# A folded bias in a graph convolution: one-row products on TensorE, or a multiply-add on VectorE from spread sums

## The reference, cut to what matters

```python
src, dst, norm = _gcn_norm(edge_index, N)      # norm = dinv[src] * dinv[dst], self loops added
h = x @ W_ae + b_ae                            # 3125 x 256 -> 3125 x 512
h = sigmoid(_gcn_conv(h, src, dst, norm, W1, b1, N))   # 512 -> 512
h = sigmoid(_gcn_conv(h, src, dst, norm, W2, b2, N))   # 512 -> 256

def _gcn_conv(h, src, dst, norm, W, b, n):
    hw = h @ W
    msg = norm[:, None] * hw[src]
    return segment_sum(msg, dst, num_segments=n) + b
```

## Time and profile before

| | before |
|---|---|
| median of 3 runs | 4179.58 us (4172.24 to 4185.87) |
| the profiled execution's own time | 4175.88 us |
| its span in the trace | 4174.1 us |
| busy: PE / PEld | 3630.8 us (87%) / 2671.5 us (64%) |
| busy: DVE / ACT / POOL | 2214.6 us (53%) / 1380.5 us (33%) / 701.9 us (17%) |
| mean granted TensorE clock | 0.92 |

### The profile page before, as it was taken

How to read it: one execution, slowest core, us unless ns; L and a number is a source line. 1 busy time by engine, 2 the same in 40 slices (tenths; PEclk the granted TensorE clock), 3 DMA queues, 4 the chain that set the end, 5 groups by cost and what they waited for, 6 DMA issues and landing times. The chain is left out here.

```text
span 4174.1 us, 91756 instructions
## 1 busy us (share of the span) xinstructions
PE 3630.8 (87%) x23927; PEld 2671.5 (64%) x23978; DVE 2214.6 (53%) x5682; ACT 1380.5 (33%) x3071; POOL 701.9 (17%) x1302
## 2 busy tenths in 40 slices
PE   4888867499979999999999997599998998799998
PEld 2444434266648967977778665498895444577776
DVE  6988877888880012115577634502106777433333
ACT  2555651377770021023210332301101253233333
POOL 3221100000000000001466632000004663000000
PEclk9999995588879998999899998699999999899999
DMA  3112220132224502520221222353351000100000
GB/s 114 46 74 79 87 110 26 41 91 84 87 78 163 195 39 102 208 91 20 73 56 49 43 64 102 125 204 123 135 206 51 1 1 5 26 8 15 12 10 31
DMA packets 121971, 320.85 MB, mean 77 GB/s; under 512 B 39597, under 2 KB 71836, under 8 KB 106554
## 3 DMA queue, kind: packets, MB, share of 16 engines
q1 hardware_dynamic: 108476, 302.94, 20.6%
q0 software_dynamic: 9936, 9.42, 1.5%
q10 hardware_dynamic: 3410, 6.54, 0.4%
HBM read 246.05 MB, written 72.96 MB: 76 GB/s over the span
## 5 line engine op out<-in xcount | busy, mean ns | idle before, releaser
L559 PE MATMUL ps<-hot_key,hot_src 128*126 128x512 bf16 (+1 forms) x2208 | 413.4, 313 | 75.7 <-DVE hot_key L524 47.4
L524 DVE TENSOR_SCALAR hot_key<-col_iota,run_keys 128x625 bf16<-128x625 int16 x1104 | 394.0, 378 | 0.0
L559 PEld LDWEIGHTS ps<-hot_key,hot_src 128*126 128x126 bf16 x2208 | 215.2, 137 | 264.7 <-DVE hot_key L524 183.0
L1365 PE MATMUL ps<-gnn_u_thirds,near 125*128 125x256 bf16 x3000 | 336.0, 275 | 13.7 <-issue 13.7
L1365 PEld LDWEIGHTS ps<-gnn_u_thirds,near 125*128 125x128 bf16 x3000 | 330.4, 141 | 16.5 <-issue 14.5
L521 DVE TENSOR_SCALAR hot_src<-col_iota,run_srcs 128x125 bf16<-128x125 int16 x828 | 212.4, 256 | 67.3 <-PE ps L559 29.1
L3773 DVE SCALAR_TENSOR_TENSOR xres<-ps,shares,xres 125x256 f32 x200 | 96.8, 484 | 244.1 <-PE ps L3738 223.3
L868 PE MATMUL ps<-row_hot,slot_hot 128*128 128x512 f16 x1088 | 221.5, 357 | 2.2 <-DVE row_hot L1081 2.2
L2542 PE MATMUL ps<-xnT,ew 128*128 (+2 forms) x640 | 181.8, 437 | 25.4 <-ACT ehT L2651 15.8
L2557 PE MATMUL ps<-ew,ehT 128*125 128x256 f32 x800 | 201.9, 396 | 0.0
L3727 PE MATMUL ps<-xnT,f 128*128 x640 | 184.6, 436 | 12.3 <-ACTq L3746 4.7
(11 more groups left out here) (595 smaller groups left out, 6743.6 us busy)
## 6 DMA issues: line engine op xcount, KB each, us to landing
near<-adjacency SPq DMA_DIRECT2D x80, 1562.5 KB, 6.5
adjacency<-counts SPq DMA_DIRECT2D x125, 312.5 KB, 2.2
own_in<-own_rows SPq DMA_DIRECT2D x34, 512.0 KB, 4.0
expert_rows<-rows_y SPq DMA_DIRECT2D x75, 125.0 KB
rows_room<-expert_rows SPq DMA_DIRECT2D x25, 375.0 KB
pair_in<-high_rows SPq DMA_DIRECT2D x34, 256.0 KB, 4.8
pair_in<-low_rows SPq DMA_DIRECT2D x34, 256.0 KB, 5.4
rows_room<-key_rows SPq DMA_DIRECT2D x8, 1024.0 KB
```

The source lines that it names most:

```text
L524: nc.vector.tensor_scalar(hot_key[:, j, :], col_iota[:], run_keys[:, ds(at, 1), j:j + 1].rearrange("p a j -> p (a j)"), None, ALU.is_equal ...
L559: last = nc.tensor.matmul(sums[:, b:e], hot_src[:, j, :], hot_key[:, j, b:e], start=False, stop=True, skip_group_check=True)
L1365: last = nc.tensor.matmul(ps[:, j, 0:width], lead_tiles[BUF[j]][:, k, :], parts.thirds[:, k, i, :], start=(k == 0 and i == 0), stop=(k == ...
```

## The change

1. `folded.b` becomes four columns on 128 partitions instead of one row of 512. PE makes them with 16 products that have `W1` as weights (128x128) and one moving column (line 665 of the changed kernel) in place of 4 products with 512 columns.
2. Ahead of the loop over groups, the node sums are spread over all partitions. DVE writes a row of 128 ones; PE multiplies it by `sT` in ten products with one row of weights (the ten halves); ACT copies the even ones and DVE the odd ones out of PSUM into `spare[:, ...]`. PE and DVE wait until all ten are out before they enter the loop.
3. In the loop the one-row product is gone. DVE adds the bias in PSUM, in place: piece += sums x folded bias (one `scalar_tensor_tensor`, 40 in all). ACT's sigmoid waits for DVE instead of PE.
4. Pieces take banks 0, 1 and 7 in turn, and a piece waits until ACT has done the one that last had its bank (`PIECE_BACK`, counted in pieces).

```diff
-        folded_b = folding.enter_context(nc.sbuf_tensor("b_ae_w1", [1, HID], F32))
+        folded_b = folding.enter_context(nc.sbuf_tensor("b_ae_w1", [128, 4], F32))
...
-                for k in range(4):
-                    last = nc.tensor.matmul(ps[0:1, 7, :], self.b_ae[:, k:k + 1], self.w1[:, k, :], start=(k == 0),
-                                            stop=(k == 3))
+                for m in range(4):
+                    for k in range(4):
+                        last = nc.tensor.matmul(ps[:, 7, m:m + 1], self.w1[:, k, m * 128:(m + 1) * 128], self.b_ae[:, k:k + 1],
+                                                start=(k == 0), stop=(k == 3))
...
-                nc.scalar.activation(self.b[:], ps[0:1, 7, :], ACT.Copy).then_inc(self.folded_out, 1)
+                nc.scalar.activation(self.b[:], ps[:, 7, 0:4], ACT.Copy).then_inc(self.folded_out, 1)
...
+                    SPREADS = [(g * NG + first, n) for g in range(G) for first, n in HALVES]
+                    SPREAD_BANKS = 6
+                    PIECE_BANK = (0, 1, 7, 0, 1, 7, 0, 1)
+                    PIECE_BACK = (2, 2, 5, 3, 3, 3, 3, 3)
+
+                    def spread_of(i):
+                        return ps[:, 2 + i % SPREAD_BANKS, 0:SPREADS[i][1]]
...
                         pe.wait_ge(landed, 32)
+                        pe.wait_ge(one_made, 1)
+                        for i, (first, n) in enumerate(SPREADS):
+                            if i >= SPREAD_BANKS:
+                                pe.wait_ge(spread_out[i % 2], (i - SPREAD_BANKS) // 2 + 1)
+                            nc.tensor.matmul(spread_of(i), one_row[:], sT[0:1, first:first + n], start=True,
+                                             stop=True).then_inc(spread_done, 1)
+                        for i in range(2):
+                            pe.wait_ge(spread_out[i], G)
                         with pe.Fori(0, G) as g:
...
-                                    pe.wait_ge(piece_out, g * 8 + (piece + 1))
-                                    o = ps[:, piece % 2, 0:n]
+                                    pe.wait_ge(piece_out, g * 8 + (piece + 9 - PIECE_BACK[piece]))
+                                    o = ps[:, PIECE_BANK[piece], 0:n]
...
-                                        nc.tensor.matmul(o, folded.w[:, c, cols], aggT[:, c, ds(g * NG + first, n)],
-                                                         start=(c == 0), stop=False)
-                                    nc.tensor.matmul(o, folded.b[0:1, cols], sT[0:1, ds(g * NG + first, n)],
-                                                     start=False, stop=True).then_inc(piece_done, 1)
+                                        last = nc.tensor.matmul(o, folded.w[:, c, cols], aggT[:, c, ds(g * NG + first, n)],
+                                                                start=(c == 0), stop=(c == 1))
+                                    last.then_inc(piece_done, 1)
...
+                        for i in range(0, len(SPREADS), 2):
+                            first, n = SPREADS[i]
+                            act.wait_ge(spread_done, i + 1)
+                            nc.scalar.activation(spare[:, first:first + n], spread_of(i), ACT.Copy).then_inc(spread_out[0], 1)
...
-                                    act.wait_ge(piece_done, g * 8 + (piece + 1))
+                                    act.wait_ge(piece_biased, g * 8 + (piece + 1))
...
+                        for i in range(1, len(SPREADS), 2):
+                            first, n = SPREADS[i]
+                            dve.wait_ge(spread_done, i + 1)
+                            nc.vector.tensor_copy(spare[:, first:first + n], spread_of(i)).then_inc(spread_out[1], 1)
+                        for i in range(2):
+                            dve.wait_ge(spread_out[i], G)
                         with dve.Fori(0, G) as g:
+                            piece = 0
+                            for first, n in HALVES:
+                                for m in range(4):
+                                    dve.wait_ge(piece_done, g * 8 + (piece + 1))
+                                    o = ps[:, PIECE_BANK[piece], 0:n]
+                                    nc.vector.scalar_tensor_tensor(o, spare[:, ds(g * NG + first, n)], folded.b[:, m:m + 1], o,
+                                                                   ALU.mult, ALU.add).then_inc(piece_biased, 1)
+                                    piece += 1
```

More of the change, by code:

```diff
@@ L1581, in graph_kernel @@
                     third_out = sem("mlp0_last_third")
+                    one_row = s("one_row", [1, 128])
+                    one_made = sem("mlp0_ones")
+                    spread_done = sem("mlp0_sums_spread")
+                    spread_out = [sem(f"mlp0_sums_out{i}") for i in range(2)]
+                    piece_biased = sem("mlp0_piece_biased")
+                    SPREADS = [(g * NG + first, n) for g in range(G) for first, n in HALVES]
[4 more added lines that the diff above has]
+                        return ps[:, 2 + i % SPREAD_BANKS, 0:SPREADS[i][1]]
                     @block.sync
@@ L1593, in _ @@
                                 for m in range(4):
-                                    pe.wait_ge(piece_out, g * 8 + (piece + 1))
-                                    o = ps[:, piece % 2, 0:n]
+                                    pe.wait_ge(piece_out, g * 8 + (piece + 9 - PIECE_BACK[piece]))
+                                    o = ps[:, PIECE_BANK[piece], 0:n]
                                     cols = slice(m * 128, (m + 1) * 128)
                                     for c in range(2):
-                                        nc.tensor.matmul(o, folded.w[:, c, cols], aggT[:, c, ds(g * NG + first, n)],
-                                                         start=(c == 0), stop=False)
-                                    nc.tensor.matmul(o, folded.b[0:1, cols], sT[0:1, ds(g * NG + first, n)],
-                                                     start=False, stop=True).then_inc(piece_done, 1)
+                                        last = nc.tensor.matmul(o, folded.w[:, c, cols], aggT[:, c, ds(g * NG + first, n)],
+                                                                start=(c == 0), stop=(c == 1))
+                                    last.then_inc(piece_done, 1)
                                     piece += 1
                             for j in range(TG):
-                                pe.wait_ge(piece_out, g * 8 + (6 if (j + 1) * P <= HALVES[0][1] else 10))
+                                pe.wait_ge(piece_out, g * 8 + (12 if (j + 1) * P <= HALVES[0][1] else 16))
                                 pe.wait_ge(rows_out, g * TG + (j + 1))
@@ L1613, in _ @@
                         act.wait_ge(landed, 32)
-                        act.sem_inc(piece_out, 2)
+                        act.sem_inc(piece_out, 8)
+                        for i in range(0, len(SPREADS), 2):
+                            first, n = SPREADS[i]
+                            act.wait_ge(spread_done, i + 1)
+                            nc.scalar.activation(spare[:, first:first + n], spread_of(i), ACT.Copy).then_inc(spread_out[0], 1)
                         with act.Fori(0, G) as g:
@@ L1618, in _ @@
                                 for m in range(4):
-                                    act.wait_ge(piece_done, g * 8 + (piece + 1))
-                                    nc.scalar.activation(h1T[:, m, first:first + n], ps[:, piece % 2, 0:n], ACT.Sigmoid,
+                                    act.wait_ge(piece_biased, g * 8 + (piece + 1))
+                                    nc.scalar.activation(h1T[:, m, first:first + n], ps[:, PIECE_BANK[piece], 0:n], ACT.Sigmoid,
                                                          bias=b1[:, m:m + 1]).then_inc(piece_out, 1)
@@ L1634, in _ @@
                     def _(dve):
+                        nc.vector.memset(one_row[:], 1.0).then_inc(one_made, 1)
                         dve.sem_inc(rows_out, TG)
-                        with dve.Fori(0, G) as g:
+                        for i in range(1, len(SPREADS), 2):
[4 more added lines that the diff above has]
+                            dve.wait_ge(spread_out[i], G)
+                        with dve.Fori(0, G) as g:
+                            piece = 0
[6 more added lines that the diff above has]
+                                    piece += 1
                             for j in range(TG + 2):
```

## The result

The changed kernel took 4136.31 us in the median of 4 runs (4133.51 to 4143.09), the kernel before 4182.73 us (4 runs, 4172.24 to 4187.76). The ratio is 0.9886, 95% interval 0.9857 to 0.9915: 46 us less, where 26 were forecast and 41 was the most that the range held. The direction was right, the size was not. The profiled execution took 4137.92 us.

What follows compares the result with a forecast made beforehand. PE's work was taken to bound the changed stage; 31.8 us saved less 7.8 us of spreading gave 24.0 us off, 4151.9 from the profiled execution or 4155.6 from the median, so 4154 us, range 4139 to 4168.

Steps and rivals of the forecast that it cites:

- What bounds the kernel: Changed stage: as long as PE's work; work given to DVE is free until DVE makes PE wait.
- The work: Changed stage: 31.8 us saved over five groups, less 7.8 us added ahead of the loop, 24.0 us off.
- The pause: Start of groups 1 to 4: PE waits 1.3 us for a bank, where it paused 0.62 us before.
- The spreading: Ahead of the loop: ten one-row products at 0.71 us, 7.1 us, plus a 0.7 us wait, 7.8 us in total.
- Rule and row: Pieces: the trace's 0.86 us saved per piece taken over the skill's rule of a third, 0.65 us.
- The clock: Changed stage: the 11.3 us lost to half clock in group 3 was left in the forecast unchanged.
- Rival 1: Changed stage keeps its full clock, so 11.3 us more go: 4141 us; chance 0.18.
- Rival 2: Spreading and its wait make the clock fall once more, costing 11 to 12 us: 4166 us; chance 0.11.
- Rival 3: Pieces lose only a third, costing 1.31 us each, so the saving is 8 us smaller: 4162 us; chance 0.08.
- Rival 4: Changed stage: pauses and waits hold the clock at half, kernel slower, past 4192 up to 4204 us; chance 0.04.
- Rival 5: Pieces: DVE's write into PSUM sets the pace at 2 us per piece, kernel about 4188 us; chance 0.03.
- The folding: Making `folded.b`: 32 MATMUL rows at 0.23 us, 7.4 us, hidden behind DVE's `own_hot`, costed at nothing.

Runs made afterwards that it cites:

- experiment 2: The changed kernel without the spreading of the node sums, the bias additions taking `aggT` instead: 4134.7 us.
- experiment 3: The kernel before with a third full product (128 rows of weights) in place of the one-row product: 4155.2 us, ratio 0.9915.
- experiment 9: The kernel before, unchanged, profiled three more times on a third chip: 4207.8, 4176.4 and 4178.2 us.
- experiment 10: The kernel before with its one-row products kept but pieces on three banks instead of two: 4162.2 us, ratio 0.9960.
- Experiment 1: The kernel before with the one-row product left out and nothing put in its place: 4147.8 us, ratio 0.9902.
- experiment 6: The changed kernel, unchanged, run and profiled again on a second chip: 4141.8 us, ratio 0.9892 to the kernel before.
- experiment 7: The changed kernel with the sums spread by the turning product of the aggregation ahead, without the ten one-row products, copies and wait: 4135.0 us.

## Why the prediction was wrong, by its own steps

**What bounds the kernel: right.** The stage was PE's, DVE's 40 additions (548 ns each, forecast 530) cost no time inside a group, and PE waits for ACT four times, 5.0 us in all. The waits of PE in the changed stage:

```profile
PE ps L1619 <- ACT h1T L1644: 5.0, 4, 1.3
PE ps L1607 <- DVE one_row L1659: 1.6, 1, 1.6
PE ps L1619 <- DVE spare L1664: 1.0, 1, 1.0
```

**The work: right, 3 us low.** Without the clock's part (11.3 us by the prediction, 4.7 by experiment 2) the stage was 141.7 - 11.3 = 130.4 us before and 108.0 - 4.7 = 103.3 after, 27.1 less for the forecast 24.0. Pieces cost 1.06 us, not the 1.10 of the expert stage, and group 0 8.51 for 8.81. The pause, 1.25, was forecast as 1.3, the group of pieces 9.94 as 10.1. Rows products became 0.11 us shorter five times. The spreading was mis-sized: I took 0.71 us for a one-row product from rows in which it stands between full ones. One behind the other they are faster. The timeline of the changed kernel shows ACT's copies of every second one, ahead of the fall:

```profile
1486.93 0.43 ACT L1638 ACTIVATE spare<-ps 128x313 f32<-128x313 f32 x1 [3.10 <-PE ps L1607]
...
1487.99 0.43 ACT L1638 ACTIVATE spare<-ps 128x313 f32<-128x313 f32 x1 [0.62 <-PE ps L1607]
...
1489.04 0.43 ACT L1638 ACTIVATE spare<-ps 128x313 f32<-128x313 f32 x1 [0.62 <-PE ps L1607]
```

They start 1.06 us apart, so one product takes 0.53 us, 5.3 in all for the 7.1 forecast. With the wait of 1.0 it is 6.3 for 7.8 at full clock; with the fall it was 8.96.

**Rule and row.** The Trainium skill (TensorE: Matmul & The Clock Gate, "Why this matters for your kernels") says that a product with 32 rows of weights takes the time of one with 128. Here, with one row, that holds where one-row products follow each other (0.53 us), since full ones take as long (0.52 to 0.53, experiment 3). Between full products it fails: 0.71 us, and the full ones beside it take 0.63 each. I was right to go by the row there, and wrong to carry it to the spreading, where the rule was right.

**The clock: the step that failed.** "The sum above leaves the loss where it is" was the sentence. Two things were wrong with it. First, the loss was no accident that would happen to both kernels: it was kept up by the one-row products between full ones, which the change removes from the pieces (experiments 3, 9 and 10), and it came behind pauses on two banks, which the change alters too (experiment 10). Second, its size was read from one profiled execution, 4175.9 us, that was among the kernel's fastest; the runs up to 4185.9 in the table beside it were the warning that the median lost more. The account of the 46 us in the medians: 27.1 work in the stage, 11.3 - 4.7 = 6.6 clock in the two profiled executions, 3.4 in the last expert stage, 0.8 net in differences elsewhere, 37.9 by the traces; then 6.8 because the profiled execution of before was that much under its median, and 1.6 because the one after was over its own. That the 6.8 are the clock in this stage is not shown. It is shown for the one long execution of experiment 9; those of 4184 to 4192 us had no profile, and their mean granted clock, 0.917 to 0.920 where it is on record, is not clearly under that of the faster ones (0.918 to 0.924). Those of 4199 us and more had 0.913 to 0.915, like the profiled long one (0.913).

**The rivals.** Rival 1 (0.18) was the nearest: full clock in the last 85 of 98 us, but priced with the one profile's 11.3 us. Rival 2 was right that the spreading brings the clock down and wrong in price, 4.7 us for 12: full pieces followed, and the clock was back 3.3 to 4.1 us after they began. I let the two exclude each other; each happened in part. Rival 3 did not happen. Rival 4 (slower) did not: pauses of 1.25 us passed at 1.00 in all four groups. The Trainium skill (TensorE: Matmul & The Clock Gate, "A second HAM failure mode: psum-queue depth-cycling"), named there, says that short pauses of PE between groups of products, on PSUM banks taken in turn, make the clock swing. Experiment 1's trace agrees, with pauses of 2.26 us on two banks and a fall after three of four; the pauses of 1.25 us on three banks had none. Rival 5 did not: 0.55 us for a write into PSUM. One sum of the chances was off: 0.86 for faster is the forecast with rivals 1 and 3 and 0.04 of rival 2's 0.11, which is not most of it.

**The folding: right, for a wrong reason.** I took 0.23 us per step from weight loads at the half clock; at full clock the 32 rows take 3.63 us, 0.11 each, hardly more than the 3.59 of the 8 before, so there was next to nothing to hide. In experiment 6, where the clock was low for their last part, they took 4.72 us and the cover was needed: PE still waited 3.24 us for `own_hot` behind them.

## What to carry to other kernels

Before pricing the removal of small products, ask what they do to those beside them: here one-row products between full ones cost 0.71 us themselves, 0.1 us on each neighbour, and kept the half clock for 24 to 31 us, where full products came out of it in 3 to 5. Ask too where PE pauses: a third bank alone took 16.7 us off the kernel before (experiment 10). When runs of one kernel spread far wider than those of its relatives, as 4170 to 4207 here against 4134 to 4143, the spread can have a place in the program; take several profiles before a price is read from one. And spread a vector over partitions inside a product that is there anyway (experiment 7), not by products of its own.

## What the hardware showed that was not expected

The fall of the clock in group 3 came 81 us after the stage's start in four of the five profiles of the kernel before, to 0.1 us, though the stage began anywhere from 1480.9 to 1487.4 us; the long execution had its falls 2, 70 and 132 us after the start.

The last expert stage, whose code is the same everywhere, took 544 to 545 us in the changed kernel (twice) and with four banks, and 548 to 550 in all others; the time at the half clock in it, 12.0 to 13.6 us, does not explain that. Its second half of pieces in a group is 4.50 us long there:

```profile
3677.23 4.50 PE L3766 MATMUL ps<-f_h1T,f 128*128 128x313 f32 x16
```

against 4.58, the same four pieces, 40 times in the stage. In 14 profiles on several chips it goes with the kernel, not with the run. Why was not tried; it is 3.4 us of the result that the change has no part in by design.
